# First attention of a four-layer kernel: query rows turned by TensorE instead of by DMA, and six loads of the expert stage issued earlier

## The reference

```
x = x + _L0_xattn_ref(_layernorm(x), ctx, ctx)     # 16 heads of width 16, softmax(q k^T / 4) v
x = x + _L0_ffn_ref(_layernorm(x), ...)            # router, 2 of 8 experts, and a shared expert
x = x + _L1_xattn_ref(_layernorm(x), ctx, ...)     # context-query attention, then a linear layer
x = x + _L1_ffn_ref(_layernorm(x), ...)            # butterfly up, gelu, butterfly down
```

## Time and profile before

| what | value |
|---|---|
| median of 3 runs | 1037.53 us (1031.3 to 1038.68) |
| the profiled execution's own time | 1036.41 us |
| its span, first to last instruction | 1034.5 us |
| granted TensorE clock, mean | 0.977 of full speed |
| first maximum of the first attention, first half of block 0 | 13.14 us |
| the same of block 31 | 192.85 us |
| end of the expert stage's products | about 674 us |

### The profile page before, as it was taken

How to read it: one execution, slowest core, us unless ns; L and a number is a source line. 1 busy time by engine, 2 the same in 40 slices (tenths; PEclk the granted TensorE clock), 3 DMA queues, 4 the chain that set the end, 5 groups by cost and what they waited for, 6 DMA issues and landing times. The chain is left out here.

```text
span 1034.5 us, 25590 instructions
## 1 busy us (share of the span) xinstructions
PE 944.8 (91%) x8802; PEld 728.9 (70%) x8802; DVE 682.7 (66%) x1586; ACT 511.1 (49%) x1076; POOL 567.3 (55%) x715
## 2 busy tenths in 40 slices
PE   3878888688999899999999999849999998999998
PEld 2555555467888566666666666538989987898997
DVE  6877888668777344445565655368899855566554
ACT  3766777634555233333333333245544536667674
POOL 7867788305774399999999932066556301100000
PEclk9989999999999999999999999969999999999999
DMA  7999999478997655445345555634544212111110
GB/s 154 227 234 200 215 209 203 114 270 270 351 331 250 186 174 187 171 153 179 85 115 124 117 130 140 117 100 137 159 129 144 82 52 62 42 56 47 41 52 32
DMA packets 206659, 156.21 MB, mean 151 GB/s; under 512 B 117744, under 2 KB 190672, under 8 KB 204752
## 3 DMA queue, kind: packets, MB, share of 16 engines
q1 hardware_dynamic: 197312, 119.99, 45.5%
q0 software_dynamic: 9232, 34.67, 10.0%
HBM read 80.03 MB, written 48.10 MB: 124 GB/s over the span
## 5 line engine op out<-in xcount | busy, mean ns | idle before, releaser
L1075 PE MATMUL Ye<-wm,hT 128*128 x852 | 105.9, 274 | 4.1 <-DMA hT<-hs 3.9
L1075 PE MATMUL Ge<-wm,xT 128*128 x426 | 104.6, 382 | 1.7 <-DVE xT L1180 1.0
L1075 PE MATMUL Ue<-wm,xT 128*128 x426 | 104.6, 382 | 0.0
L1075 PEld LDWEIGHTS Ye<-wm,hT 128*128 128x128 f16 x852 | 83.6, 98 | 28.6 <-issue 4.9
L1936 ACT ACTIVATE gf<-H,bup,wdesc 128x256 f32<-128x256 f32 x128 | 71.9, 564 | 56.1 <-DVE g L1909 33.0
L394 DVE TENSOR_REDUCE nmx<-S 128x8 bf16<-128x1024 f32 x64 | 78.1, 1221 | 31.7 <-PE S L531 31.5
L1965 PE MATMUL H<-T6s,wm 128*128 128x256 f16 x768 | 94.7, 274 | 4.2 <-DVE T6s L1904 2.6
L1407 POOL DMA_INDIRECT yg<-ys_d,slot x64 | 66.5, 1039 | 54.1 <-DMA ys_d<-ye 36.7
L1977 PE MATMUL Y<-wm,g 128*128 128x256 f16 x768 | 94.8, 274 | 0.7 <-DVE g L1909 0.7
L1909 DVE SCALAR_TENSOR_TENSOR g<-gf,g 128x512 f16<-128x512 f32 x64 | 44.5, 696 | 72.1 <-ACT g L1941 72.1
L1965 PEld LDWEIGHTS H<-T6s,wm 128*128 128x128 f16 x768 | 75.2, 98 | 13.8 <-DVE T6s L1904 2.9
(11 more groups left out here) (291 smaller groups left out, 2373.2 us busy)
## 6 DMA issues: line engine op xcount, KB each, us to landing
stage<-in_L_ffn_W_dram SPq DMA_DIRECT2D x24, 512.0 KB, 7.2
xs_d<-zeros SPq DMA_DIRECT2D x36, 256.0 KB, 4.1
ys_d<-ye SPq DMA_DIRECT2D x71, 128.0 KB, 2.0
xe<-xs_d SPq DMA_DIRECT2D x69, 128.0 KB, 2.5
bw<-in_L_ffn_up_weights_dram POOLq DMA_DIRECT2D x7, 1024.0 KB, 6.5
bw<-_L_ffn_down_weights_dram POOLq DMA_DIRECT2D x7, 1024.0 KB, 5.3
xb<-in_x_dram SPq DMA_DIRECT2D x16, 256.0 KB, 3.8
cb<-in_ctx_dram SPq DMA_DIRECT2D x16, 256.0 KB, 3.6
```

The source lines that it names most:

```text
L1075: last = nc.tensor.matmul(bank, left[:, xp, c, :], wm[:, kind, bass.ds(e, 1), wp, c * width:(c + 1) * width], start=i == 0 and c == 0, sto ...
```

## The change

It has two parts.

**Queries.** The DMA transpose of `qs` goes. PE turns it by eight half-precision transposes per block (`queries`) into a new bank `T` of PSUM, and ACT copies the 1024 columns to `qT` (`turned_queries`), which is now two deep. To make room for `T`, the two banks of the turned maxima `TM` become one, with a wait more in `shifts`. The keys are still turned by DMA, and the low half of the second norm (`second_low`) is still on ACT. A half-precision identity is made at the start.

**Loads.** The six loads of 256 KB that were issued together at tile 65 of the expert stage are now issued one per tile at tiles 10 to 15.

```
@@ first attention, SP
                             sp.dma_start_transpose(kT[:, t % 3, :, :], ks[:, t % 2, :, :, :].rearrange("p h l d -> p (h l d)")
                                                    ).then_inc(s_kT[t % 2], 16)
-                            sp.wait_ge(s_ql, t + 1)
-                            sp.dma_start_transpose(qT[:, t % 3, :, :], qs[:, t % 2, :, :, :].rearrange("p h l d -> p (h l d)")
-                                                   ).then_inc(s_qT[t % 2], 16)
@@ first attention, ACT
+                    def turned_queries(t):
+                        if 0 <= t < NB:
+                            act.wait_ge(s_tq, t + 1)
+                            if t >= 2:
+                                act.wait_ge(s_st1, 2 * t - 2)
+                            A.copy(qT[:, t % 2, :, :], T[:, :, :]).then_inc(s_eq, 1)
...
                         exponents(t, 1)
+                        turned_queries(t + 2)
                         router(t - 3)
                         shift(t + 1, 0)
@@ first attention, PE
+                    def queries(t):
+                        if 0 <= t < NB:
+                            pe.wait_ge(s_qh, t + 1)
+                            pe.wait_ge(s_ql, t + 1)
+                            if t >= 1:
+                                pe.wait_ge(s_eq, t)
+                            for i in range(HH):
+                                last = nc.tensor.transpose(
+                                    T[:, i, :], qs[:, t % 2, 2 * i:2 * i + 2, :, :].rearrange("p h l d -> p (h l d)"),
+                                    identh[:, :])
+                            last.then_inc(s_tq, 1)
...
                     def scores(t, h):
                         if 0 <= t < NB:
-                            pe.wait_ge(s_qT[t % 2], 16 * (t // 2 + 1))
+                            pe.wait_ge(s_eq, t + 1)
...
                     def shifts(t, h):
                         if 0 <= t < NB:
                             pe.wait_ge(s_mx, 2 * t + h + 1)
-                            if t >= 1:
-                                pe.wait_ge(s_em[h], t)
-                            MM(TM[h], nmx[:, h, :, :].rearrange("p g j -> p (g j)"), identb[:, :], start=True,
+                            if h == 1:
+                                pe.wait_ge(s_em[0], t + 1)
+                            elif t >= 1:
+                                pe.wait_ge(s_em[1], t)
+                            MM(TM[:, h, :], nmx[:, h, :, :].rearrange("p g j -> p (g j)"), identb[:, :], start=True,
...
-                    for t in range(-1, NB + 2):
+                    for t in range(-2, NB + 2):
                         scores(t + 1, 0)
+                        queries(t + 2)
                         values(t, 0)
@@ expert stage, SP
-                        if t == NE - 6:
+                        if t == 10:
                             for j in range(2):
                                 sp.wait_ge(s_ast[j], 16 * (NP // 2))
-                            for p in range(3):
-                                sp.dma_start(ax[:, p, :, :], pair(acc_d, p)).then_inc(s_ax[p], 16)
-                                sp.dma_start(cx[:, p, :, :], pair(ctx_in, p)).then_inc(s_cx[p], 16)
+                        if 10 <= t < 13:
+                            sp.dma_start(ax[:, t - 10, :, :], pair(acc_d, t - 10)).then_inc(s_ax[t - 10], 16)
+                        if 13 <= t < 16:
+                            sp.dma_start(cx[:, t - 13, :, :], pair(ctx_in, t - 13)).then_inc(s_cx[t - 13], 16)
```

More of the change, by code:

```diff
@@ L154, in build_program @@
             ks = sb("ks", [P, 2, NH, 4, DH], F16)
-            qT = sb("qT1", [P, 3, HH, P], F16)
+            qT = sb("qT1", [P, 2, HH, P], F16)
             kT = sb("kT1", [P, 3, HH, P], F16)
@@ L168, in build_program @@
             negh = sb("negh", [P, P], F16)
+            identh = sb("identh", [P, P], F16)
             identb = sb("identb", [P, P], BF16)
@@ L175, in build_program @@
             M = ps_("M", [P, 4, P])
-            TM = [ps_(f"TM{h}", [P, 4, P])[:, 0, :] for h in range(2)]
+            T = ps_("T", [P, HH, P], F16)
+            TM = ps_("TM", [P, 4, P])
             Ov = O[:, :, :].rearrange("p s (c d) -> p (s c) d", d=2 * DH)
@@ L183, in build_program @@
             s_ks, s_va = sem("s_ks"), sem("s_va")
-            s_qT, s_kT = sems("s_qT", 2), sems("s_kT", 2)
+            s_tq, s_eq, s_kT = sem("s_tq"), sem("s_eq"), sems("s_kT", 2)
             s_sc, s_mx, s_tm, s_st1, s_exp, s_pv, s_oe, s_ot = (
@@ L192, in build_program @@
             s_x1st, s_h1Tst = sems("s_x1st", 2), sems("s_h1Tst", 2)
-            CONSTS, FILLED = 11, NB // 2
+            CONSTS, FILLED = 12, NB // 2
             heads = lambda a: a.rearrange("p (h d) -> p h d", h=NH)
@@ L361, in _ @@
                     V.tensor_scalar(negh[:, :], ident[:, :], -1.0 / XS, None, ALU.mult).then_inc(s_c, 1)
+                    V.tensor_copy(identh[:, :], ident[:, :]).then_inc(s_c, 1)
                     V.tensor_copy(identb[:, :], ident[:, :]).then_inc(s_c, 1)
@@ L462, in shift @@
                                 act.wait_ge(s_st1, 2 * t - 1 + h)
-                            A.copy(mT[:, h, :], TM[h]).then_inc(s_em[h], 1)
+                            A.copy(mT[:, h, :], TM[:, h, :]).then_inc(s_em[h], 1)
                     def turned_values(t):
@@ L491, in query_high @@
                             if t >= 2:
-                                act.wait_ge(s_qT[t % 2], 16 * (t // 2))
+                                act.wait_ge(s_tq, t - 1)
                             A.copy(qs[:, t % 2, :, 0:2, :],
                                    heads(xn[:, t % 2, :]).unsqueeze(2).broadcast_to([P, NH, 2, DH])).then_inc(s_qh, 1)
+                    def turned_queries(t):
[4 more added lines that the diff above has]
+                            A.copy(qT[:, t % 2, :, :], T[:, :, :]).then_inc(s_eq, 1)
                     act.wait_ge(s_k0, 2)
@@ L530, in scores @@
                                     rows = slice(g * P // 2, (g + 1) * P // 2)
-                                    last = MM(S[:, g, j, :], qT[rows, t % 3, HP2 * h + j, :], kT[rows, t % 3, HP2 * h + j, :],
+                                    last = MM(S[:, g, j, :], qT[rows, t % 2, HP2 * h + j, :], kT[rows, t % 3, HP2 * h + j, :],
                                               start=True, stop=True)
@@ L552, in scores_turned @@
                                     rows = slice(g * P // 2, (g + 1) * P // 2)
-                                    MM(ST[:, g, j, :], kT[rows, t % 3, HP2 * h + j, :], qT[rows, t % 3, HP2 * h + j, :],
+                                    MM(ST[:, g, j, :], kT[rows, t % 3, HP2 * h + j, :], qT[rows, t % 2, HP2 * h + j, :],
                                        start=True, stop=False)
```

## The result

The change made the kernel slightly slower. The medians are 1038.45 us with the change (1036.31 to 1041.03) and 1033.9 us before it (1029.86 to 1038.68), 15 runs each; the ratio is 1.0035, with an interval from 1.002 to 1.0051. I had forecast 1026 us, 1.1% less. The time lies within the range, but it moved the other way.

A forecast was written before the change was run, and what follows sets the result against it. No engine was saturated in the first attention, where dependences through four engines set the pace; PE bound the expert stage. Terms -5.8 - 10.7 + 8.4 - 1.1 - 1.0 = -10.2 us took 1036.4 to 1026 us, range 1018 to 1042.

The forecast's parts named there:

- ring, 31 steps: First attention: PE transposes and ACT copy lengthen the four-engine dependence cycle by 0.27 us per step, +8.4 us.
- waits for queries: First attention: scores no longer wait for the queries' DMA transpose; 13.5 us less 2.8 kept for late keys, -10.7 us.
- last three steps: End of the first attention: ACT's extra weight copy adds 0.37 us per step instead of 0.73, -1.1 us.
- start: First attention's first scores no longer wait for a DMA of queries behind one of keys, -1 us.
- loads (whole expert stage): Expert stage: moving six loads from tile 65 removes PE's wait for a DMA transpose and its aftermath, -5.8 us.
- My walk: First attention, event by event along the dependences: turned maxima at 1.96 instead of 1.72 us, next scores at 5.54.
- the choice of the limiting engine: First attention: the first copy of maxima comes at 2.42 instead of 1.98 us, behind ACT's copy of `T` and logits.
- steps of over 5.9 us: Sign of being wrong: at such step times the first attention brings a loss.
- a step above 7 us: Sign in the first attention's maxima: none this long was expected except at the 512 KB loads.
- My sentence on this wait: First attention: POOL's rest of the queries ends at 0.69 us; only then can PE's transposes start, at about 0.74.
- The ring without overlap: Rival, chance 0.15: first attention's links do not overlap, steps take 6.12 us, total 1044 us.
- PE's clock: Rival, chance 0.06: in the first attention the granted clock falls, 0.93 us more per step, total 1055 us.

The follow-up runs named there:

- small copy: The changed kernel with ACT copying, from block 2 on, only 128 of the 1024 columns of `T`; 1038.22 us, ratio 1.004 to the kernel before.
- one transpose: The changed kernel with PE making, from block 1 on, only the first of the eight transposes, full copy kept; 1028.53 us, ratio 0.9944 to the kernel before.
- the loads alone: The kernel before with only the six loads moved to tiles 10 to 15; 1031.92 us, ratio 0.9963 to the kernel before.
- transposes without the copy: The kernel before, loads at tile 65, plus eight unused PE transposes; queries still come by DMA; 1044.31 us, ratio 1.0106 to the kernel before.
- queries only: The changed kernel with the six loads put back to tile 65; 1039.82 us, ratio 1.006 to the kernel before.
- the transposes stand between the values: The changed kernel with PE's eight transposes moved between the two halves of the values; 1036.18 us, or 1032.4 us with ACT's logits also ahead of the copy.
- the queries a block earlier: Queries made one block earlier: PE version from the changed kernel, 1020.6 us; DMA version from the kernel before with loads moved, 1034.98 us.

## Why the prediction was wrong

Each term against what the two traces show:

| term | forecast us | measured us |
|---|---|---|
| ring, 31 steps | +8.4 | +19.2 |
| waits for queries | -10.7 | -9.7 |
| last three steps | -1.1 | -1.9 |
| start | -1.0 | +1.0 |
| loads (whole expert stage) | -5.8 | -4.4 |
| sum | -10.2 | +4.2 |

The marks give +4.5; the rest is rounding and one step of 5.96 us.

**The ring was mis-sized; this is the step that failed.** My walk had the order of events right, but let PE reach the turned maxima at 1.96 us. They came at 2.35. Of the 0.39 us, 0.06 are the start of the transposes (0.80, not 0.74), 0.08 their time on PE (131.47 - 130.93 = 0.54, not 0.46), 0.05 the weight loads of the values (0.81, not 0.76), and 0.20 an idle time between values and turned maxima, which I did not have at all. Before, PE stood 0.39 us at this point and waited for DVE's maxima, so that it could not be seen. In all, the kernel before had 0.64 us of idle time on PE's way to the turned maxima, 0.25 ahead of the second half of the values and those 0.39. The change put 1.27 us in: the values start 1.02 us later (1.34, not 0.32), 0.05 are their weight loads and 0.20 the idle time. Of these, 0.64 took the place of the old idle time, and the other 0.63 us lengthened the step.

With this went the choice of the limiting engine. I had the first copy of maxima wait for ACT (2.42) with PE 0.2 us beneath. In fact it waits for PE (2.62), and ACT would have been ready at about 2.49 (the logits start at 2.35, and 0.14 more as in my walk). The small copy shows it: it freed ACT and moved nothing. The 3.55 us from turned maxima to next scores came out nearly as I walked them (3.58, with the copy's 0.03 in it). Forecast 1.96 with a step of 5.54, the kernel with one transpose has 1.96 and 5.50: the walk was good, its input was not. I had named steps of over 5.9 us as the point from which the first attention brings a loss. That was a slip: by my own terms it gains 10.7 + 1.1 + 1.0 = 12.8 us beside the ring, so that it breaks even at 5.27 + 12.8 / 31 = 5.68 us, and 5.87 is where the whole sum comes to nothing. Had I put 2.35 into the walk, the sum would have been -10.2 + 31 x (0.62 - 0.27) = +0.6 us, no change.

**The start** has a cost where I had a gain: 2.3 us more of irregular steps, less the 1.2 us by which the first maxima are earlier. The next steps take 8.75 and 6.41 us, although I had named a step above 7 us there as a sign of being wrong. PE takes its instructions in order, so that the transposes of block 1, which wait for POOL's rest, hold up the turned maxima and second scores of block 0 behind them. My sentence on this wait looked at the undisturbed step only.

**The waits for queries** went nearly as forecast. 3.8 us stay at the 512 KB loads (8.64 + 6.94 - 2 x 5.89), where I kept 2.8, and the keys are what PE waits for, as I had said. That the number is so close is in part luck: in the profile of the loads alone the same first attention takes 182.0 us from block 0 to 31 instead of 179.7, so that this term is known to about 2 us only. But the term is not a gain beside the ring's cost: in the kernel of transposes without the copy more than half of the same waits vanish in the longer step.

**The loads** removed their hole as said (4.12 us at its tiles). Measured by medians, they are worth 3.8 us (1.2 to 6.3) rather than 5.8: the hole was 5.8 us in the one profile that I had read. In the other two profiles with late loads it was 2.0 us (6.07 - 4.12, queries only) and 2.5 us (6.59 - 4.12, transposes without the copy).

**The last three steps** are 6.00 us, as before, and pay 0.11 over their neighbours instead of 0.73: the longer step hides the weight copies.

**Rivals.** The ring without overlap (0.15) had the right sign and size, 6.12 us, for a wrong reason: the joints do overlap as I walked them. PE's clock did not fall: 1.00 in the undisturbed step, 0.983 over the whole span (0.977 before). The Trainium skill (TensorE: Matmul & The Clock Gate, Part 4) says that transposes don't count as PE-busy in the same way; eight more of them per step left the clock alone here, beside the other products. The 275 ns that the Trainium skill gives for a transpose (the same part) is not the distance of two in this kernel: a single one lasts 0.22 us (the kernel with one transpose), and eight take 0.61 us together.

**What can be told apart.** I had written that less than 1% can't be told from no change. With 15 runs of each kernel the interval is 0.3% wide, and the +0.35% is clear of it.

## What to carry to other kernels

Where no engine is full, follow one engine's queue from the ring's start to the instruction that releases the next link, add up what stands between, small idle gaps too, and compare it with the slack that the queue had; the step grows by what is beyond the slack. Work that moves to another engine belongs in that engine's idle place, with its operands made far enough ahead that it never waits: the same transposes and copy cost 0.62 us per step in one place and nothing in another. A wait removed and a step lengthened are not two terms to be summed, since a longer step hides the wait by itself.

## What the runs showed of the hardware

- Behind a group of values (single-precision products with 32 columns of weights) PE stood idle 0.20 us ahead of the next group, though nothing that it waits for was late: in the changed kernel, with the small copy, with one transpose, and twice per step where the transposes stand between the values. Behind the second norm's half-precision product the same transposes followed without a gap. What causes it was not tested.
- Eight half-precision 128x128 transposes take 0.54 us of PE's time, and ACT's copy of their 1024 half-precision columns from PSUM 1.01 us, of which 0.91 count (132.48 - 131.57).
- A DMA transpose of 128x1024 halves that was issued right behind 1.5 MB of loads landed 6.7 us (keys, before), 7.8 us (keys, with the change) and 8.6 and 8.8 us (keys, in the two kernels with the queries a block earlier, by PE and by DMA) after its issue, and one of queries 4 us behind these loads after 7.3 us; the fastest landings were at 3.0 us.
